# Sorting the tokens of three of ten blocks by expert, and taking a stage's order from a list schedule

## Chip, cores and metric

The kernel runs on one core of a Trainium2 chip. The metric is the time of one execution on the device in microseconds (us), as a median of several runs. Beside the runs there is one execution recorded by the hardware profiler: its span is the time from its first to its last instruction.

## What is computed

A network of four layers over 2500 nodes (padded to 2560 rows, 20 tiles of 128) of 256 features and 40000 edges: a relational graph layer, a mixture of 6 experts, a graph attention layer with a feed-forward part, and a mixture of 8 experts. Each is added to its input. The change touches the second layer and the stage that it shares with the first:

```python
# first layer, per edge: a row of a table by source node and edge type, summed by destination node
H = jnp.einsum('ni,rio->nro', x, W)
agg = jax.ops.segment_sum(H[src, etypes], dst, num_segments=N_NODES)
...
# second layer: top 2 of 6 experts per node, each expert three products of 256 x 256
rh = jax.nn.relu(features @ router_w1 + router_b1)
expert_logits = jax.nn.softmax(rh @ router_w2 + router_b2, axis=-1)
top_w, top_i = jax.lax.top_k(expert_logits, TOP_K)
routing_weights = jax.nn.softmax(top_w, axis=-1)
h1 = jax.nn.relu(jnp.einsum('bsd,edh->bseh', features, expert_w1) + expert_b1)
h2 = jax.nn.relu(jnp.einsum('bseh,ehf->bsef', h1, expert_w2) + expert_b2)
expert_out = jnp.einsum('bsef,efo->bseo', h2, expert_w3) + expert_b3
sel = jnp.take_along_axis(expert_out, top_i[:, :, :, None], axis=2)
combined = jnp.sum(sel * routing_weights[..., None], axis=2)
```

`features` is the normalized sum of the node's input and the first layer.

## The kernel before

The program runs stages one after the other with a barrier between them: loading, the table of the first layer (`stage_tables`), the stage of the change (`stage_sums_experts`), and the attention stage, which also holds the last experts. A second run of `stage_sums_experts` with `redo` stands behind a condition and does not happen on these inputs.

`stage_sums_experts` holds two streams of work on the same engines. The first is 79 groups of 4 tiles of 128 edges. For each tile POOL issues one indirect gather of 128 rows of 1 KB from the table in DRAM (L1149), into a ring of 16 tiles, four groups. PE multiplies each gathered tile by a 0/1 matrix of the destinations (L1466) into one PSUM bank, `psG`; below group 50 it also adds the last row of the group before (L1464, "follow"). ACT copies one half out of the bank (`odd`, L1400), DVE adds the other (`halves`, L1215), SP stores the sum to the table `agg` in DRAM (`store`). From group 50 on POOL joins the first row by a DMA that accumulates (L1144, `join`).

The second stream is ten blocks of 256 nodes. Block b can start when group 8(b+1) is stored (the last after group 78); `READY_AFTER` lists these groups. SP loads the block's sums, DVE normalizes (`norm`, `normed`, with ACT's `std` between), PE transposes (`turn`), and the router follows: `hidden`, `logits`, `gates` (softmax and top 2 on DVE and ACT), `gateT`, `bias`. The experts are dense: each of the 6 experts is applied to every token of the block, as pieces A, B and C (first, second and third product) of four products of 128x128 by 256 columns. In float32 each product stands in the trace as two PE records, so a piece is 8 records. ACT evicts A and B with bias and relu (L1387), DVE evicts C, weighted by the gate, into an accumulator (`sum_expert`, L1309). The block's tail normalizes twice (`post`, `post1`, `post2`), transposes (`turn2`), projects to queries, keys and values (`q`, L1517, one piece per tile), splits the queries into three bf16 parts (`high`, `rest`, `mid`, `low`) and stores.

Every engine works its queue in order. The order of the pieces on PE, DVE, ACT and SP is written out by hand: `BEGIN0` says at which group each block begins, `PACE0` how many groups one unit of its pattern lasts, and `BLOCK0` gives each piece a place in the pattern; `order0` sorts all pieces by the resulting place. POOL simply issues gathers and joins. PSUM is divided by use: `psG` one bank for the groups, `psW` two for router, turns and projections, `psH` three for A and B, `psC` two for C; the last block's second projection uses `psH`.

## Time and profile before

| | us |
|---|---|
| median of 3 runs | 1725.58 |
| lowest and highest run | 1723.24, 1728.3 |
| span of the profiled execution | 1668.6 |
| its PE busy | 1495.7 |
| its VectorE (DVE) busy | 1028.6 |
| its GpSimd (POOL) busy | 781.2 |
| its ScalarE (ACT) busy | 615.6 |

The profiled execution has no time of its own among the runs; its span lies 57.0 us under the median. Busy time is the time in which an engine had an instruction under way. PE is the matmul engine, PEld its weight loads, SP the engine that issues most DMAs. The clock of a stretch is what the throttle granted to PE, 1.00 for 2.4 GHz and 0.50 for 1.2 GHz. In a timeline a row is one instruction or a run of like ones, and the bracket behind it says how long the engine was idle ahead of it and what ended that.

### The profile page before, as it was taken

To read this page: it belongs to the slowest core of one execution; us is meant where nothing else is said; L and a number is where in the kernel's file an instruction comes from. 1 tells how busy PE (TensorE), PEld (TensorE's weight loads), DVE (VectorE), ACT (ScalarE), POOL (GpSimd) and SP (SyncE) were. 2 spreads that over 40 slices of the span, in tenths; PEclk is the share of its full clock that TensorE was granted. 3 is DMA by queue.
4 is the path that set the end of the run, shared out by engine and by line. 5 is a ranking of instruction groups with operands and counts; after the bars stand their busy time and mean duration, and the time that the engine had idled before them with its cause. 6 is when DMAs were issued, how large, how long until landed. Compare 5 with 4: busy or idle time off the path is not lost. (4 is left out here: it accounts for less than half of the span.)

```text
span 1668.6 us, 23723 instructions
## 1 busy us (share of the span) xinstructions
PE 1495.7 (90%) x6795; PEld 1005.9 (60%) x6795; DVE 1028.6 (62%) x2542; ACT 615.6 (37%) x1534; POOL 781.2 (47%) x738
## 2 busy tenths in 40 slices
PE   4999788999999999998356799999999999999996
PEld 2554314665666777777233467767766767767785
DVE  6543244345445555545388789898898888896432
ACT  3121002333234343443022355554555445555341
POOL 1100277646755777600378666574746556540000
PEclk9999857999999999999556699999999999999997
DMA  8448456546766566631487885665757565641100
GB/s 258 164 161 261 142 151 172 154 115 191 213 175 180 166 190 178 164 94 47 137 252 216 267 253 165 193 180 167 208 152 212 143 196 169 179 122 39 29 7 9
DMA packets 191573, 270.07 MB, mean 162 GB/s; under 512 B 28295, under 2 KB 156035, under 8 KB 188867
## 3 DMA queue, kind: packets, MB, share of 16 engines
q1 hardware_dynamic: 148419, 144.77, 27.7%
q0 software_dynamic: 43008, 123.61, 26.8%
q8 instruction: 60, 0.98, 0.2%
q14 instruction: 86, 0.70, 0.1%
HBM read 196.22 MB, written 72.06 MB: 161 GB/s over the span
## 5 line engine op out<-in xcount | busy, mean ns | idle before, releaser
L1890 POOL DMA_INDIRECT att_kv<-table_kv,g_srcI x314 | 368.5, 1174 | 246.4 <-issue 180.4
L1149 POOL DMA_INDIRECT ex_hg<-table_h,z_idx x314 | 316.7, 1008 | 150.2 <-issue 84.9
L2441 PE MATMUL att_psR<-g_mw,att_h 128*128 128x256 f32 x640 | 163.9, 403 | 1.0 <-ACT att_h L2259 1.0
L2414 PE MATMUL att_psR<-att_t,g_mw 128*128 128x256 f32 (+1 forms) x640 | 154.8, 387 | 0.1
L1466 PE MATMUL ex_psG<-ex_hg,ex_oh 128*42 128x256 f32 x628 | 134.6, 427 | 13.3 <-DMA ex_hg<-table_h,z_idx 7.2
L751 PE MATMUL tab_psH<-e_u,tab_xT 128*128 128x512 f32 x320 | 142.6, 598 | 4.3 <-DVE e_u L532 4.3
L2441 PEld LDWEIGHTS att_psR<-g_mw,att_h 128*128 128x128 f32 x640 | 124.7, 200 | 23.0 <-ACT att_h L2259 4.0
L1387 ACT ACTIVATE ex_h<-ex_psH,g_cols 128x256 f32<-128x256 f32 (+1 forms) x240 | 97.3, 464 | 93.8 <-PE ex_psH L1488 93.1
L2414 PEld LDWEIGHTS att_psR<-att_t,g_mw 128*128 128x128 f32 x640 | 121.2, 199 | 16.6 <-issue 2.6
L1882 POOL DMA_DIRECT2D table_o<-att_part x59 | 54.2, 919 | 161.9 <-DMA table_o<-att_part 90.5
L2301 PE MATMUL att_psG<-att_kv,att_oh 128*42 128x264 f32 x628 | 109.5, 431 | 13.7 <-DVE att_kv L1997 13.3
L1910 DVE TENSOR_TENSOR att_kv<-att_kv,att_epb 128x1024 f32<-128x1024 f32 x79 | 96.4, 1220 | 39.9 <-DMA att_kv<-table_kv,g_srcI 32.9
L1501 PE MATMUL ex_psC<-e_experts,ex_h 128*128 128x256 f32 x480 | 114.0, 384 | 0.0
L1488 PE MATMUL ex_psH<-ex_xT,e_experts 128*128 128x256 f32 (+1 forms) x480 | 113.8, 380 | 0.1
L1215 DVE TENSOR_TENSOR ex_part<-ex_psG,ex_odd 42x256 f32<-42x256 f32 x79 | 32.5, 411 | 130.6 <-ACT ex_odd L1400 130.4
L1488 PE MATMUL ex_psH<-ex_h,e_experts 128*128 128x256 f32 (+1 forms) x480 | 111.6, 377 | 0.0
L2259 ACT ACTIVATE att_h<-att_psR,g_cols 128x256 f32<-128x256 f32 (+1 forms) x160 | 66.2, 464 | 116.8 <-PE att_psR L2414 116.4
L2105 DVE SCALAR_TENSOR_TENSOR att_acc<-att_psR,att_gate,att_acc 128x256 f32<-128x256 f32 x160 | 69.5, 475 | 59.8 <-PE att_psR L2441 59.8
L751 PEld LDWEIGHTS tab_psH<-e_u,tab_xT 128*128 128x128 f32 x320 | 60.8, 192 | 74.3 <-issue 71.0
L1501 PEld LDWEIGHTS ex_psC<-e_experts,ex_h 128*128 128x128 f32 x480 | 88.9, 190 | 19.6 <-issue 7.2
L1997 DVE TENSOR_TENSOR att_kv<-att_kv,att_p 128x1024 f32<-128x1024 f32 x79 | 95.5, 1209 | 7.0 <-ACT att_p L2212 6.9
L1488 PEld LDWEIGHTS ex_psH<-ex_xT,e_experts 128*128 128x128 f32 x480 | 87.7, 190 | 17.6 <-issue 7.7
(308 smaller groups left out, 2465.1 us busy)
## 6 DMA issues: line engine op xcount, KB each, us to landing
table_h<-tab_hs SPq DMA_DIRECT2D x20, 1024.0 KB, 4.0
att_eft<-in_eft SPq DMA_DIRECT2D x158, 64.0 KB
ex_db<-table_dst SPq DMA_DIRECT2D x79, 126.0 KB
table_ohT<-ex_ohT SPq DMA_DIRECT2D x79, 126.0 KB
att_ohT<-table_ohT SPq DMA_DIRECT2D x79, 126.0 KB
table_oh<-ex_oh SPq DMA_DIRECT2D x79, 84.0 KB, 2.3
att_oh<-table_oh SPq DMA_DIRECT2D x79, 84.0 KB, 4.0
table_kv<-ex_qkv SPq DMA_DIRECT2D x10, 512.0 KB, 4.8
```

The source lines that it names most:

```text
L751: ins = nc.tensor.matmul(psH[:, c % 4, :], xT[:, b % 2, k, q * P:(q + 1) * P], Wr[:, k, j * 512:(j + 1) * 512], start=(k == 0), stop=(k == ...
L1149: nc.gpsimd.indirect_dma_start(hg[:, t % RING0, :], None, d.h[:, :], bass.IndirectOffsetOnAxis(ap=g.idx0[:, t:t + 1], axis=0)).then_inc(go ...
L1387: nc.scalar.activation((h1 if what == "A" else h2)[:, e % 2, o, 0:used(b)], psH[:, n % 3, o * BLK0:o * BLK0 + used(b)], ACT.Relu, bias=vec ...
L1466: ins = nc.tensor.matmul(psG[at:at + WG, 0:D], oh[:, i % 3, t % TP, :], hg[:, t % RING0, :], start=(t <= second), stop=(t >= tiles(i)[-1] ...
L1488: ins = nc.tensor.matmul(psH[:, n % 3, o * BLK0:o * BLK0 + w_], w[:, e, k, o * P:(o + 1) * P], x[:, k, 0:w_], start=(k == 0), stop=(k == D ...
L1501: ins = nc.tensor.matmul(psC[:, e % 2 * BT0 + q, :], h2[:, e % 2, k, q * P:(q + 1) * P], g.w3[:, e, k, :], start=(k == 0), stop=(k == DK - 1))
L1890: nc.gpsimd.indirect_dma_start(kv[:, t % (RINGC * TP), H:H + 2 * D], None, d.kv[:, :], bass.IndirectOffsetOnAxis(ap=g.srcI[:, t:t + 1], ax ...
L1910: nc.vector.tensor_tensor(k, k, epb[:, i % 2, :, :].unsqueeze(2).to_broadcast([P, TP, H, DH]), ALU.add).then_inc(s.added, 1)
L1997: nc.vector.tensor_tensor(kv[:, b:b + TP, 0:H * VW].rearrange("p t (a c) -> p t a c", c=VW)[:, :, :, 0:DH], kv[:, b:b + TP, H + D:H + 2 * ...
L2301: ins = nc.tensor.matmul(psG[at:at + WG, 0:H * VW], oh[:, i % 3, t % TP, :], kv[:, t % (RINGC * TP), 0:H * VW], start=(t <= second), stop= ...
L2414: ins = nc.tensor.matmul(out[:, c * CB:c * CB + used(b)], g.mw1[:, e, k, c * P:(c + 1) * P], t3[:, k, 0:used(b)], start=(k == 0), stop=(k ...
L2441: ins = nc.tensor.matmul(out[:, q * D:(q + 1) * D], h1[:, n % 3, k, q * P:(q + 1) * P], g.mw2[:, e, k, :], start=(k == 0), stop=(k == DK - 1))
```

## The change

Blocks 4, 5 and 6 no longer apply all six experts to all tokens. Their 768 tokens are each written twice, once for each chosen expert, into a table `sorted_x` in DRAM, sorted by expert: DVE marks the choices, PE counts them with products by a triangular and an all-ones matrix (`rank`), DVE makes positions (`pos`), and POOL scatters the normalized rows by indirect DMAs (`scatter`, four per block). The table is cut into 17 slots of 128 rows of one expert each, 2 x 768 / 128 + 6 - 1, the most that can be needed; all 17 always run. DVE makes a table of each slot's expert and first row (`table`), PE loads the expert numbers into registers (`experts`), SP loads the slots (`sL`). For each slot PE transposes the rows (`sX`), multiplies them by the expert's weights, addressed by the register (`sA`), transposes (`tA`), multiplies (`sB`), transposes (`tB`), multiplies (`sC`); ACT evicts the transposes, with bias and relu for `tA` and `tB`, and DVE evicts the products. SP stores each slot's result (`sS`) to `sorted_y`, POOL fetches for each token its two rows (`fetch`, four per block), and DVE adds them with their gates (`combine`). The table `sorted_x` is set to zero in the stage before, by DMAs of SP beside the stores of the first layer's table (5376 rows of 1 KB; two tiles of 128 rows at a time, eight at the last).

The other seven blocks stay dense, but C is added straight into `x` (`sum_expert`) and the mixed biases are added by DVE first (`mixed`); the accumulator and `addx` go. The gates are split into `shift`, `exp`, `choose`, `exp2` and `mix`.

PSUM is divided anew: five banks `psR` are handed out piece by piece for everything but the groups and the projections, which keep `psG` and `psW`; PE waits for the piece that held the bank before (`take`). The last block's projections have `psW` alone. The tile `u` is reused for sums (two deep), `u2` (two deep), the fetched rows and the loaded slots (four deep). The loads of destination rows (`db`) are three deep instead of two.

The order is no longer written by hand. `pieces0` gives each piece a cost, a rank and the pieces it needs; `plan0` puts them in order, always the piece that could start first, and among equals the lowest rank. POOL's order now comes from it too. SP's `store` is split into `store`, `keep` and `sums`.

```diff
+                    if tile >= 2:
+                        each = SXROWS // P // (NT - 2)
+                        n = each if tile < NT - 1 else SXROWS // P - (NT - 3) * each
+                        at = (tile - 2) * each * P
+                        sp.dma_start(d.sx[at:at + n * P, :].rearrange("(t p) c -> p t c", p=P),
+                                     zero[:, 0:D].unsqueeze(1).to_broadcast([P, n, D])).then_inc(cleared, 16)
...
+DENSE0, PARTS0 = (0, 1, 2, 3, 7, 8, 9), ((4, 5, 6),)
...
+SLOTS0 = [2 * cap // P + E0 - 1 for cap in CAP0]
...
+XR, YR, DB = 4, 2, 3
...
 
 
...
+COST0 = {"gather": 5.0, "join": 1.25, "scatter": 5.0, "fetch": 5.0,
+         "group": 1.66, "turn": 0.62, "hidden": 1.05, "logits": 0.52, "rank": 0.35, "gateT": 0.38, "bias": 0.90,
+         "experts": 1.20, "sX": 0.31, "sA": 0.96, "tA": 0.31, "sB": 0.96, "tB": 0.31, "sC": 0.96, "A": 1.90, "B": 1.90, "C": 1.90, "turn2": 0.62, "q": 2.90}
...
+RANK0 = {"route": 2.1, "slots": 7.5, "pace": 1.0, "dense": 45.6, "post": 59.2, "fetch": 4.4}
...
+        at = 8.0 * b + RANK0["dense"]
...
+            add("PE", "A", b, e, at + e, after("ACT", "turn", b), after("PE", "sC", AT0[slots_before[-1] + 1] - 1, slots_before[-1]) if slots_before else after("", "", -1))
...
+            add("PE", "B", b, e, at + e - 0.5, after("ACT", "A", b, e))
...
+            add("PE", "C", b, e, at + e - 0.7, after("ACT", "B", b, e))
...
+        at = 8.0 * part[-1] + RANK0["slots"]
...
+            add("SP", "sL", n, p, at + RANK0["pace"] * j, prior("PE", "sX", XR), after("DVE", "table", p), *(after("POOL", "scatter", b, 0, LANDS) for b in part))
+            add("PE", "sX", n, p, at + RANK0["pace"] * j - 0.3, after("SP", "sL", n, p, LANDS), prior("PE", "sX", 1), after("PE", "experts", p),
+                *(after("PE", "C", b, E0 - 1) for b in DENSE0 if b < part[0]))
+            add("ACT", "sX", n, p, at + RANK0["pace"] * j, after("PE", "sX", n, p), prior("PE", "sA", 2))
+            add("PE", "sA", n, p, at + RANK0["pace"] * j, after("ACT", "sX", n, p), prior("PE", "sA", 1))
...
+            add("PE", "tA", n, p, at + RANK0["pace"] * j - 0.5, after("DVE", "sA", n, p))
...
+            add("PE", "sB", n, p, at + RANK0["pace"] * j - 0.6, after("ACT", "tA", n, p), prior("PE", "sB", 1))
...
+            add("PE", "tB", n, p, at + RANK0["pace"] * j - 0.7, after("DVE", "sB", n, p))
...
+            add("PE", "sC", n, p, at + RANK0["pace"] * j - 0.8, after("ACT", "tB", n, p), prior("PE", "sC", 1))
+            add("DVE", "sC", n, p, at + RANK0["pace"] * j - 20.0, after("PE", "sC", n, p), prior("SP", "sS", YR, LANDS))
+            add("SP", "sS", n, p, at + RANK0["pace"] * j - 20.0, after("DVE", "sC", n, p))
...
+            add("POOL", "fetch", b, 0, at + RANK0["fetch"], *(after("SP", "sS", m, p, LANDS) for m in range(AT0[p], AT0[p + 1])),
...
+        best = None
+        for engine, pieces in open_.items():
+            for piece in pieces:
+                start = max(free[engine], ready[piece])
+                if engine == "PE" and piece[1] in HELD0:
+                    start = max(start, min(banks))
+                if start < float("inf") and (best is None or (start, work[piece][1]) < best[0]):
+                    best = ((start, work[piece][1]), piece)
...
+        engine, what, b, e = piece
...
+        end = free[engine] = start + work[piece][0]
+        orders[engine].append((what, b, e))
+        if engine == "PE" and what in HELD0:
+            n = min(range(5), key=lambda n: banks[n])
+            bank[what, b, e], behind[what, b, e] = n, holder[n]
...
+        sums_in = g.u[:, 0:2 * BT0, :].rearrange("p (a t) c -> p a t c", t=BT0)
+        u2 = g.u[:, 2 * BT0:4 * BT0, :].rearrange("p (a t) c -> p a t c", t=BT0)
+        yf = g.u[:, 4 * BT0:8 * BT0, :].rearrange("p (a t j) c -> p a t j c", t=BT0, j=2)
+        xs = g.u[:, 8 * BT0:8 * BT0 + XR, :]
...
-        psH = m.ps("psH", [P, 3, 512])
-        psC = m.ps("psC", [P, 2 * BT0, D])
...
+        psR = m.ps("psR", [P, 5, 512])
...
+                for p, part_of in enumerate(PARTS0):
+                    nc.gpsimd.iota(g.first0[:, p, :], [[CAP0[p], E0]], base=AREA0[p], channel_multiplier=0, allow_small_or_imprecise_dtypes=True)
+                    nc.gpsimd.iota(g.row0[:, AT0[p]:AT0[p + 1]], [[P, SLOTS0[p]]], base=AREA0[p], channel_multiplier=0,
+                                   allow_small_or_imprecise_dtypes=True)
+                nc.gpsimd.iota(g.turn0[:, :], [[1, SL]], base=0, channel_multiplier=0, allow_small_or_imprecise_dtypes=True).then_inc(s.places, 1)
...
+                def scatter(b):
+                    pool.wait_ge(s.pos_ready, sparse(b) + 1)
+                    pool.wait_ge(s.xn_ready, b + 1)
...
+                    for q in range(B0[b]):
+                        for j in range(2):
+                            nc.gpsimd.indirect_dma_start(d.sx[:, :], bass.IndirectOffsetOnAxis(ap=pos[:, T0[b] + q, j:j + 1], axis=0),
+                                                         xn[:, b % 2, q, :], None).then_inc(scattered[PART0[b]][b % 2], 16)
...
+                for what, b, e in orders["POOL"]:
+                    if what == "gather":
+                        if b * TP >= RING0:
+                            pool.wait_ge(s.summed, b - RING0 // TP + 1)
+                        for t in tiles(b):
+                            nc.gpsimd.indirect_dma_start(hg[:, t % RING0, :], None, d.h[:, :],
+                                                         bass.IndirectOffsetOnAxis(ap=g.idx0[:, t:t + 1], axis=0)).then_inc(got[t % RING0], 16)
+                    if what == "join":
...
+                def keep_first(n):
+                    dve.wait_ge(s.sa_made, n + 1)
+                    if n >= 2:
+                        dve.wait_ge(s.ta_made, n - 1)
+                    nc.vector.tensor_copy(ha[:, n % 2, :], psR[:, bank["sA", n, PART_OF[n]], 0:D]).then_inc(s.sa_kept, 1)
...
+                def take(what, b, e):
+
+                    if behind[what, b, e]:
+                        pe.wait_ge(*drained(*behind[what, b, e]))
+                    return None if what == "q" else psR[:, bank[what, b, e], :]
...
+                def turn_slot(what, n, p, src, made):
+                    out = take(what, n, p)
+                    for k in range(DK):
+                        ins = nc.tensor.transpose(out[:, k * P:(k + 1) * P], src[:, k * P:(k + 1) * P], g.ident[:, :])
+                    ins.then_inc(made, 1)
+
+                def layer_slot(what, n, p, x, w, made):
+                    out = take(what, n, p)
+                    for k in range(DK):
+                        ins = nc.tensor.matmul(out[:, 0:D], x[:, n % 2, k, :], w[:, ds(expert[n], 1), k, :].rearrange("p a c -> p (a c)"),
+                                               start=(k == 0), stop=(k == DK - 1))
+                    ins.then_inc(made, 1)
...
+                        if what == "sX":
+                            pe.wait_ge(x_got[b % XR], 16 * (b // XR + 1))
+                            turn_slot(what, b, e, xs[:, b % XR, :], s.xs_made)
+                        if what == "sA":
+                            pe.wait_ge(s.xs_ready, b + 1)
+                            layer_slot(what, b, e, xsT, g.w1, s.sa_made)
...
+                        if what == "sL":
+                            if b == AT0[e]:
+                                sp.wait_ge(s.table_ready, 3 * e + 1)
+                                for j in range(2):
+                                    sp.wait_ge(scattered[e][j], scatters(e, PARTS0[e][-1], j))
+                                settle(sp)
+                            at = sp.value_load(tabR[0:1, b:b + 1], min_val=0, max_val=SXROWS - P)
+                            if b >= XR:
+                                sp.wait_ge(s.xs_made, b - XR + 1)
+                            sp.dma_start(xs[:, b % XR, :], d.sx[ds(at, P), :]).then_inc(x_got[b % XR], 16)
+                        if what == "sS":
+                            sp.wait_ge(s.y_ready, b + 1)
+                            sp.dma_start(d.sy[e][(b - AT0[e]) * P:(b - AT0[e] + 1) * P, :], y[:, b % YR, :]).then_inc(y_stored[b % YR], 16)
```

## Rows read from the trace of the kernel before

**Rows 1.** The page: the span and the busy time of each engine.

```profile
span 1668.6 us, 23723 instructions
...
PE 1495.7 (90%) x6795; PEld 1005.9 (60%) x6795; DVE 1028.6 (62%) x2542; ACT 615.6 (37%) x1534; POOL 781.2 (47%) x738
```

**Rows 2.** Busy time of each engine in four stretches (window: length, engines with counts, clock, DMA).

```profile
core 0: us, PE busy (x) PEld busy (x) DVE busy (x) ACT busy (x) POOL busy (x), PEclk, DMA share, GB/s
220.00:240.00 20.00, 16.15 (x43) 4.11 (x44) 9.32 (x46) 1.48 (x4) 15.43 (x16) 0.50 0.59 154
275.00:700.00 425.00, 419.30 (x1966) 283.03 (x1965) 205.39 (x683) 156.87 (x361) 276.51 (x279) 1.00 0.60 172
700.00:790.00 90.00, 86.00 (x420) 69.44 (x418) 46.20 (x147) 36.81 (x86) 4.91 (x6) 1.00 0.25 76
790.00:800.00 10.00, 2.27 (x6) 1.38 (x7) 5.50 (x18) 1.61 (x4) 0.00 (x0) 0.70 0.15 52
```

**Rows 3.** Timeline of PE near 610 us (start, length, engine, line, operation, count).

```profile
604.92 1.07 PE L1466 MATMUL ex_psG<-ex_hg,ex_oh 128*42 128x256 f32 x8
605.91 1.99 PE L1501 MATMUL ex_psC<-e_experts,ex_h 128*128 128x256 f32 x8
607.74 0.60 PE L365 MATMUL ex_psW<-g_ident,ex_xn 128*128 128x128 f32 x4
...
617.40 1.99 PE L1488 MATMUL ex_psH<-ex_h,e_experts 128*128 128x256 f32 x8
619.23 1.89 PE L1488 MATMUL ex_psH<-ex_xT,e_experts 128*128 128x256 f32 x8
```

**Rows 4.** Timeline of PE near 400 us: a group below 50, and what follows it.

```profile
400.06 1.06 PE L1466 MATMUL ex_psG<-ex_hg,ex_oh 128*42 128x256 f32 x6
...
402.13 1.99 PE L1488 MATMUL ex_psH<-ex_xT,e_experts 128*128 128x256 f32 x8
```

**Rows 5.** Timeline of POOL: the iota, the first and the fiftieth gather of the stage.

```profile
194.31 0.93 POOL L1134 IOTA ex_qrow<- 128x126 f32 x1 [46.94 <-POOLq L813]
195.41 1.32 POOL L1149 DMA_INDIRECT ex_hg<-table_h,z_idx  x1 [0.17 <-issue]
...
261.03 1.51 POOL L1149 DMA_INDIRECT ex_hg<-table_h,z_idx  x1 [0.30 <-issue]
```

**Rows 6.** DMA issues by tensor (count, size of one, median us to landing).

```profile
table_h<-tab_hs SPq DMA_DIRECT2D x20, 1024.0 KB, 4.0
...
ex_hg<-table_h,z_idx POOLq DMA_INDIRECT x314, 3.6
...
att_x<-table_x SPq DMA_DIRECT2D x10, 256.0 KB, 3.3
```

**Rows 7.** Timelines of ACT, PE and DVE: routing of the first and of the last block.

```profile
249.25 0.37 ACT L1400 COPY ex_odd<-ex_psG 42x256 f32<-42x256 f32 x1 [4.89 <-PE ex_psG L1466]
...
264.76 1.06 PE L365 MATMUL ex_psW<-g_ident,ex_xn 128*128 128x128 f32 x4
...
748.06 0.60 PE L365 MATMUL ex_psW<-g_ident,ex_xn 128*128 128x128 f32 x4
...
754.69 0.17 DVE L933 TENSOR_TENSOR ex_r_p<-ex_psW,g_rows 128x12 f32<-128x12 f32 x1 [0.79 <-PE ex_psW L1573]
...
759.50 0.16 DVE L1258 TENSOR_TENSOR ex_r_m<-ex_r_m 128x2 f32<-128x2 f32 x1
```

**Rows 8.** Timeline of PE: the end of the stage.

```profile
786.22 3.62 PE L1501 MATMUL ex_psC<-e_experts,ex_h 128*128 128x256 f32 x16
796.53 1.12 PE L365 MATMUL ex_psW<-g_ident,ex_xn 128*128 128x128 f32 x4 [6.69 <-DVE ex_xn L1231]
798.85 5.46 PE L1517 MATMUL ex_psW<-z_wqkv,ex_x2T 128*128 128x512 f32 x8 [1.20 <-ACT ex_x2T L1433]
804.10 2.79 PE L1517 MATMUL ex_psH<-z_wqkv,ex_x2T 128*128 128x512 f32 x8
```

748 lines of the change are left out of this document (570 added, 178 removed), and 5 rows, old and new, of the table BLOCK0.

## The prediction

> **What bounds the kernel now.** I read four views in this order. The page gives a span of 1668.6 us with PE busy 90% of it, the next engine at 62% [rows 1], so the question is where PE works and where it waits. Busy time by stretch answers it for the stage that the change rewrites, which runs from about 194 us (first iota) to about 817 us: from 275 to 700 us PE is busy 419.3 of 425 us, from 700 to 790 us 86.0 of 90 us, both at clock 1.00 (2.4 GHz) [rows 2]. So this stage is bound by PE's work from 275 us on, with 9.7 us of holes in 515. Ahead of 275 us PE waits for gathers: in 220 to 240 us it does groups alone at clock 0.50 (1.2 GHz), while POOL issues one gather after the other [rows 2]. Behind 790 us the last block's chain runs through DVE and ACT, and PE has 2.3 us of work in 10 us. Stretches outside this stage are untouched but for zero stores in the stage ahead of it. The third view, PE's timeline, prices the pieces; the fourth, POOL's timeline with the landings of transfers, says when a block can start.
>
> The median of the runs is 1725.58 us, 57.0 us above the span; I carry those 57 us over unchanged and sum against the span.
>
> **What the change takes from PE.** A dense piece is 8 records and goes from start to start in 1.83 us: a C from 605.91 to 607.74, a B from 617.40 to 619.23 [rows 3]. A block has 18 of them, 32.9 us; three blocks lose 98.8 us.
>
> **What it adds to PE.** Seventeen slots, each three layers of 4 records (half of 1.83, 0.92 us) and three turns of 2 transposes (half of the 0.60 us of four [rows 3], 0.30 us): 3.66 us, 62.2 us for all. Operands addressed by a register are not in the trace. From below they cost nothing, since the address could be resolved while the array streams; from above I take 0.3 us per layer piece, the pause that a POOL instruction shows ahead of itself without waiting for anything (0.30 <-issue [rows 5]), 15 us in all. I take 0, because PE's records here follow each other without a gap [rows 3] and the address is known long before. Three rankings and the load of 17 expert numbers are some 2.4 us (a ranking is shorter than a group's 0.99 us, 604.92 to 605.91; 0 to 5 us). Net PE work: -98.8 + 62.2 + 2.4 = **-34.2 us**. Routing, biases, projections and groups stay.
>
> **The start.** Three iotas go ahead of the first gather; the present one takes 0.93 us and 0.17 us pass after it [rows 5]. Three like it are 3.3 us; they are shorter, 17 columns at most, so I take **+2.2 us** (1 to 3.3). This stretch waits for POOL, so it counts in full.
>
> **The hole before the slots.** Slots share their buffers with the dense blocks, so no slot starts before block 3's last C, and no A of block 7 before the last slot's sC. And none starts before block 6, the third of the part, is sorted. Two times must be compared.
>
> When does PE run out of dense work? Groups have rank i and dense block 0 rank 45.6, so PE takes a group whenever one is ready. A group below 50 holds PE 2.07 us (400.06 to 402.13 [rows 4]), a later one 0.99 us. The fiftieth gather starts at 261.03, the first at 195.41, 1.34 us apart [rows 5]; from 220 to 240 us there are 16, 1.25 us apart [rows 2]. A group's four are 5.0 to 5.4 us; I take 5.3. Group 49 lands near 195.4 + 2.2 + 50 x 5.3 + 3.6 = 466 us (3.6 us to landing [rows 6]). From 275 us PE has 1 - 2.07/5.3 = 61% for blocks, 116 us until then. Four blocks need 4 x 42.3 us: 32.9 dense, 6.2 for the tail (four transposes 0.60, two projections of 2.79 [rows 3, 8]), some 3.2 for routing, an estimate from the same pieces. With the routing of blocks 4 and 5 that is 175 us. The remaining 59 us run at 84% (0.99 us per 6.3 us, a join of 1.2 added): dense work ends near **537 us**.
>
> When can the first slot start? Group 56 needs 57 x 5.3 = 302 us of gathers, the scatters of blocks 4 and 5 (eight indirect issues, priced as gathers, 10.6 us) and three joins (3.7 us): it lands near 518 us with its PE work. From a group's odd half to block 0's turn it took 15.5 us (249.25 to 264.76 [rows 7]), part of it behind other DVE work, and a join adds some 4 us: 17.5 us. Turn to logits took 6.6 us beside other pieces (748.06 to 754.69), alone some 3.8; the gate's choice takes 5.0 us (754.69 to 759.66 [rows 7]); ranking and positions 2; the scatter 5.3 and 3.6 to land; the slot's load 0.4 and 3.3 [rows 6]. Together 40 us: **558 us**.
>
> The gap is 21 us, in which groups (16%) and block 6's own routing (3.3 us) occupy PE: **+15 us** idle, from 0 (dense work 4% dearer and the chain 5 us shorter close it) to 30 (the slower pieces of each pair).
>
> Behind the hole the slot pipeline fills: a slot passes PE, ACT and DVE six times in turn, so the first gives PE some 5 us of holes, **+5 us** (2 to 10). PE's clock falls in such holes: after 6.69 us of idle the projection at 798.85 took 5.46 us, the next one 2.79 [rows 8], **+2.7 us**. The Trainium skill, "TensorE: Matmul & The Clock Gate", section "What's actually happening", says that the throttled clock is the default and that activity releases it; rows 2 and 8 agree (0.50 with groups alone, 0.70 over the end). [...]
>
> **The order.** PE's holes were 1.3% from 275 to 700 us and 4.4% from 700 to 790 [rows 2]. The new order comes from a list of fixed costs that puts each piece where it is just ready, with no slack: 5.0 us for four gathers against 5.3 here, 1.66 us for each group against 2.07 and 0.99. I take 3% of 480 us, 14.5 against 9.7: **+5 us** (-4 to +15). New waits sit here: a scatter waits on POOL with all later gathers behind it, the first slot's load waits on SP with stores and sums behind it. Both have four groups of ring and four partial sums in front; if that cover is gone a late scatter delays the next group one for one.
>
> **The end.** Block 8's tail has rank 123.2, behind all of block 9's dense pieces (122.6 at most), so its projections (5.6 us) can fall into the 6.69 us in which PE waited for the last block's norm, and the last projection then finds a fast clock (2.7). Against it, the last block has no second projection bank any more: its second projection waits some 1.2 us for DVE. **-6 us** (-8 to +1.2).
>
> **Counted as nothing:** 5.5 MB of zeros in the stage ahead, beside PE, whose h stores of 1 MB land in 4.0 us [rows 6]; the last zero store is 1 MB, so up to 4 us if it queues in front of the last h store. DVE's and ACT's 51 small evictions each and 12 fetches on POOL lie beside PE; DVE was busy 205 of 425 us, ACT 157 [rows 2].
>
> Sum: -34.2 + 2.2 + 15 + 5 + 2.7 + 5 - 6 = **-10.3 us**, 1725.6 - 10.3 = **1715.3 us**; span near 1658.
>
> **Rivals.** *No hole.* If block 6 is sorted when block 3 ends, 15 and 2.7 us go: -28 us, **1697 us**. For it: the two times are 21 us apart out of 540, and 0.2 us per group closes half. Against: the 5.3 us per group were measured with PE and DVE at light work.
>
> *Groups late (slower than before).* The hole grows if groups come later than each 5.3 us; each 0.1 us is 5.7 us on block 6 and 4.8 us of PE idle, since PE runs out at nearly the same time. From 5.5 us per group on nothing is gained. From 275 to 700 us POOL ran 279 instructions [rows 2], some 26 of them joins: 63 groups, 6.7 us each, but there PE was the limit. At 5.9 us the sum is +18 us: **1744 us**. For it: each group waits for ACT's odd half and DVE's sum before the next may use its one bank, and both queues hold long pieces now.
>
> *Slots bound by hand-overs.* If a slot takes 4.6 us instead of 3.66, because bank, ACT copy and DVE copy don't come in time, or because registers cost their upper bound, 15 to 16 us come back: **1731 us**, about no change. For it: two buffers per step. Against: five banks, and groups and tails to fill in.
>
> *The work isn't cut*: were experts so uneven that 17 slots did not hold all tokens, the kernel would be wrong; 17 is the most that can be needed, and all 17 always run, so this can't move the time.
>
> **Chances.** Forecast 0.45, no hole 0.19, groups late 0.21, hand-overs 0.15. A measurement tells 0.3% (5.2 us) from no change. Faster takes 0.39 of the forecast, all of no hole and 0.02 of hand-overs: 0.60. Within 0.3%: 0.05, 0.03 of groups late, 0.07 of hand-overs: 0.15. Slower: 0.25. The range reaches from no hole with a clean order, 1694, to groups late, 1745; the forecast's own is 1704 to 1726.
>
> **What would show it.** PE has some 120 records fewer (432 dense gone, 204 layer and 102 turn records and a few more added). The hole: PE idle or at a clock below 1.00 somewhere in 530 to 570 us, ended by a slot's transpose waiting for its load. Groups: the 57th group's gather near 515 us. Slots: 17 in 62 to 75 us. The end: the stage over near 807 instead of 817 us, its last projection at 2.8 us. The prediction is wrong if the hole is elsewhere, for instance at each group, or if PE waits at pieces whose order the list put too early.

## The result and the profile after

| | before | changed |
|---|---|---|
| median of the runs, us | 1724.41 (4 runs) | 1773.66 (4 runs) |
| lowest and highest run | 1707.03, 1728.3 | 1767.1, 1777.17 |
| span of the profiled execution | 1668.6 [rows 1] | 1772.6 |
| its time as a run | none | 1775.16 |

The ratio is 1.0307 (95% interval 1.0262 to 1.0351): some 49 us slower where 10 us faster was forecast, and outside the range of 1694 to 1745. The page of the changed kernel, against [rows 1]: PE has about as much modelled work as before (1501.1 us against 1495.7) and a longer span.

```profile
span 1772.6 us, 24123 instructions
...
PE 1501.1 (85%) x6676; PEld 995.1 (56%) x6676; DVE 1050.6 (59%) x2630; ACT 611.2 (34%) x1539; POOL 791.5 (45%) x765
```

Its busy time by stretch, against [rows 2]: from 275 to 700 us PE works 364 of 425 us instead of 419, at clock 0.92 instead of 1.00.

```profile
core 0: us, PE busy (x) PEld busy (x) DVE busy (x) ACT busy (x) POOL busy (x), PEclk, DMA share, GB/s
220.00:240.00 20.00, 5.25 (x16) 1.68 (x17) 5.91 (x28) 0.74 (x2) 11.79 (x13) 0.50 0.37 109
275.00:700.00 425.00, 364.26 (x1597) 223.16 (x1595) 192.75 (x696) 129.27 (x307) 262.71 (x271) 0.92 0.61 173
700.00:890.00 190.00, 164.47 (x746) 124.50 (x744) 94.42 (x275) 64.32 (x156) 44.82 (x47) 0.94 0.32 95
```

POOL's timeline of the changed kernel gives the stage's length, from the first iota to the first gather of the attention stage: 704.6 us. In the first trace of the kernel before it is 623 us (194.31, [rows 5], to 817.55).

```profile
194.84 0.94 POOL L1364 IOTA ex_qrow<- 128x126 f32 x1 [46.94 <-POOLq L833]
...
899.46 1.07 POOL L2417 DMA_INDIRECT att_kv<-table_kv,g_srcI  x1 [120.57 <-issue]
```

So by the traces the stage is 81 us longer, but by the runs the program is only 49 us longer. That mismatch was the first thing to settle.

### The profile page after: what moved, and what is told of

Same layout as the page of the kernel before. It is cut to its first block and busy times, and to the rows that moved or that the text cites. A ratio compares the mean times of both kernels' runs of the same rounds, so it can differ in the third digit from the quotient of the medians.

```text
span 1772.6 us, 24123 instructions
## 1 busy us (share of the span) xinstructions
PE 1501.1 (85%) x6676; PEld 995.1 (56%) x6676; DVE 1050.6 (59%) x2630; ACT 611.2 (34%) x1539; POOL 791.5 (45%) x765
## 5 line engine op out<-in xcount | busy, mean ns | idle before, releaser
L2417 POOL DMA_INDIRECT att_kv<-table_kv,g_srcI x314 | 363.9, 1159 | 298.0 <-issue 209.8
L1407 POOL DMA_INDIRECT ex_hg<-table_h,z_idx x314 | 308.1, 981 | 185.0 <-PE ex_psG L1936 83.3
L1936 PE MATMUL ex_psG<-ex_hg,ex_oh 128*42 128x256 f32 x628 | 140.2, 439 | 54.1 <-issue 47.8
L1835 ACT ACTIVATE ex_h<-ex_psR,g_cols 128x256 f32<-128x256 f32 (+1 forms) x168 | 69.1, 463 | 152.5 <-PE ex_psR L1951 77.0
L1936 PEld LDWEIGHTS ex_psG<-ex_hg,ex_oh 128*42 128x42 f32 x628 | 44.8, 127 | 128.6 <-issue 108.3
L1951 PE MATMUL ex_psR<-ex_h,e_experts 128*128 128x256 f32 (+1 forms) x336 | 85.5, 402 | 22.7 <-ACT ex_h L1835 21.4
L2442 DVE TENSOR_TENSOR att_kv<-att_kv,att_psQ 128x1024 f32<-128x1024 f32 x79 | 95.3, 1206 | 13.5 <-DMA ex_db<-table_dst 13.4
L1848 ACT COPY ex_odd<-ex_psG 42x256 f32<-42x256 f32 x79 | 29.1, 369 | 211.3 <-PE ex_psG L1936 112.8
L1424 DVE TENSOR_TENSOR ex_oh<-g_iotag,g_dstgrp 128x168 f32<-128x168 f32 x79 | 25.7, 328 | 120.4 <-PE ex_psG L1936 52.8
L2448 DVE TENSOR_REDUCE att_S<-att_kv 128x32 f32<-128x1024 f32 x79 | 95.5, 1209 | 0.9
```

The lines of the kernel that those rows point to most:

```text
L1407: nc.gpsimd.indirect_dma_start(hg[:, t % RING0, :], None, d.h[:, :], bass.IndirectOffsetOnAxis(ap=g.idx0[:, t:t + 1], axis=0)).then_inc(go ...
L1936: ins = nc.tensor.matmul(psG[at:at + WG, 0:D], oh[:, i % 3, t % TP, :], hg[:, t % RING0, :], start=(t <= second), stop=(t >= tiles(i)[-1] ...
L2417: nc.gpsimd.indirect_dma_start(kv[:, t % (RINGC * TP), H:H + 2 * D], None, d.kv[:, :], bass.IndirectOffsetOnAxis(ap=g.srcI[:, t:t + 1], ax ...
L2442: nc.vector.tensor_tensor(keys(i), keys(i), psQ[:, :, :], ALU.mult).then_inc(s.product, 1)
L2448: nc.vector.tensor_reduce(heads(i), keys(i).rearrange("p t (a c) -> p t a c", c=DH), AX.X, ALU.add).then_inc(s.reduced, 1)
```

## Experiments

All ratios are to the kernel before, run on the same chip beside the kernel. The rows come from five chips, on which the kernel before had medians of 1722.7 to 1730.7 us, so a difference of a few us between rows of different chips says little by itself; the ratio then tells more.

| run | median us | ratio, 95% interval | stage us |
|---|---|---|---|
| kernel before, again | 1730.86 (one run) | | 661.0 |
| changed kernel, again | 1779.49 (one run) | | 707.5 |
| list alone (all dense) | 1753.38 | 1.0209, 1.0139 to 1.0279 | 687.0 |
| halves first | 1765.5 | 1.0256, 1.0188 to 1.0325 | 702.0 |
| halves first, prices by shape | 1757.66 | 1.0147, 1.0107 to 1.0187 | 694.4 |
| list alone, both of these | 1747.51 | 1.0118, 1.0067 to 1.0170 | 679.5 |
| slots late (blocks 6 to 8) | 1762.16 | 1.0182, 1.0148 to 1.0217 | 696.5 |
| slots late, both of these | 1738.93 | 1.0059, 1.0023 to 1.0094 | 665.0 |
| the same with two group banks | 1738.71 | 1.0072, 1.0036 to 1.0109 | 677.0 |
| two banks, blocks 7 and 8 sorted | 1732.13 | 1.0026, 0.9997 to 1.0055 | 672.9 |
| two banks, list alone | 1743.89 | 1.0085, 1.0040 to 1.0130 | 680.1 |
| one bank, blocks 7 and 8 sorted | 1723.81 | 1.0006, 0.9974 to 1.0038 | 651.9 |
| before, plain loads, first run | 1680.08 (one run) | | 607.8 |
| before, plain loads | 1679.17 | 0.9724, 0.9665 to 0.9782 | 611.4 |
| changed, plain loads | 1674.6 | 0.9692, 0.9638 to 0.9745 | 612.3 |
| list alone, plain loads | 1697.42 | 0.9813, 0.9748 to 0.9878 | 627.2 |
| slots late and both, plain loads | 1649.79 | 0.9549, 0.9480 to 0.9617 | 585.8 |

### Both kernels once more

No edit.

> The kernel before once more, unchanged, for a second trace of it: the first one has a span of 1668.6 us under a median of runs of 1725. If that first execution was an unusually quick one, the span here is near 1705 to 1725 us and the stage of sums and experts lasts longer than its 623 us (194 to 817). If not, the span is again near 1669 and 55 us lie outside it. In the trace of the changed kernel 102 signals of PE in this stage reach their reader over 0.3 us after the modelled end of the matmul (3.0 us on average), in the first trace of the kernel before none of 421. If late signals are a property of the executions, they are here too, and with them holes of PE of some 40 us more; if they come from the change, there are none.

> The changed kernel once more, unchanged. First trace: stage from 194 to about 895 us, PE holes of 160 us in it, first slot at 638.4, one hole of 12.6 us at 232 and one of 13 us at 755, 102 late signals of PE. If these holes belong to the order of the pieces, they come again at the same places (2.5 us at each group from 239 to 288, 10 us at the second product of the first dense block behind the slots); if they belong to that execution, they are elsewhere or gone. Time 1767 to 1777 us either way.

The second trace of the kernel before has a span of 1729.3 us in a run of 1730.86: 1.6 us lie outside it, not 57. Its page, its stretches and POOL's two rows:

```profile
span 1729.3 us, 23723 instructions
...
220.00:240.00 20.00, 8.99 (x24) 2.48 (x24) 6.06 (x29) 0.96 (x3) 12.20 (x13) 0.50 0.40 111
275.00:700.00 425.00, 402.31 (x1826) 264.86 (x1825) 191.27 (x638) 143.37 (x330) 253.89 (x255) 0.97 0.57 160
700.00:800.00 100.00, 95.86 (x470) 75.06 (x468) 54.17 (x186) 41.66 (x98) 30.99 (x33) 1.00 0.42 125
...
193.87 0.93 POOL L1134 IOTA ex_qrow<- 128x126 f32 x1 [46.92 <-POOLq L813]
...
854.90 1.08 POOL L1890 DMA_INDIRECT att_kv<-table_kv,g_srcI  x1 [92.96 <-issue]
```

The stage lasts 661 us here, 38 more than in the first trace, and the attention stage 874 instead of 851. From 275 to 700 us PE stands 22.7 us, where [rows 2] have 5.7. The first trace was of an execution whose span is some 36 us shorter than the shortest that a timed run of that kernel has (1704.5). The fair difference between the stages is 706 - 661 = 45 us, close to the 49 of the medians.

Where PE stands shows in timelines, first PE and ACT of the kernel before, second trace. A group ends at 468.81 + 0.63 = 469.44 us; ACT, idle, takes its odd half only at 472.35.

```profile
468.81 0.63 PE L1466 MATMUL ex_psG<-ex_hg,ex_oh 128*42 128x256 f32 x2
469.37 1.99 PE L1488 MATMUL ex_psH<-ex_xT,e_experts 128*128 128x256 f32 x8
471.20 1.89 PE L1501 MATMUL ex_psC<-e_experts,ex_h 128*128 128x256 f32 x8
...
472.35 0.37 ACT L1400 COPY ex_odd<-ex_psG 42x256 f32<-42x256 f32 x1 [5.83 <-DMA table_x<-e_x]
```

PE's signal came 2.9 us late, and PE lost nothing, because the hand-written order gave it an A and a C in between. The same in the changed kernel: a group ends at 484.25 + 0.63 = 484.88, ACT takes its half at 488.59, 3.7 us late ("remote": the signal came long after its sender's end).

```profile
484.25 0.63 PE L1936 MATMUL ex_psG<-ex_hg,ex_oh 128*42 128x256 f32 x2
485.88 1.99 PE L1951 MATMUL ex_psR<-ex_h,e_experts 128*128 128x256 f32 x8 [1.01 <-issue]
489.61 1.07 PE L1936 MATMUL ex_psG<-ex_hg,ex_oh 128*42 128x256 f32 x6 [1.74 <-issue]
...
484.99 0.84 ACT L1835 ACTIVATE ex_h<-ex_psR,g_cols 128x256 f32<-128x256 f32 x2 [3.70 <-remote]
488.59 0.37 ACT L1848 COPY ex_odd<-ex_psG 42x256 f32<-42x256 f32 x1 [2.76 <-remote]
...
489.10 0.41 DVE L1476 TENSOR_TENSOR ex_part<-ex_psG,ex_odd 42x256 f32<-42x256 f32 x1
```

Here PE stands twice, 1.01 and 1.74 us: the list has put the B right behind the relu it needs, and the next group right behind the sum that frees the bank. I call a signal late when an engine's signal comes over 0.3 us (and under 9 us) after the modelled end of the matmul that sends it and its reader starts on it. Counted over the stage: none of 421 in the first trace of before, 71 in the second, 102 and 104 in the two of the changed kernel, 3 to 4 us late on average. In the attention stage, which is the same in both programs: none in the first trace of before, 93, 81 and 92 in the others. These counts depend on how the reader is told (another way gives 62 and 112 where 71 and 102 stand), but none stays none. The holes of the changed kernel returned (some 121 and 122 us from PE's first to its last instruction of the stage, against 67 in the second trace of before), with the 2.5 us at each group in the same place.

The traces with late signals differ from the others in one more way: they lack records of signals. From 275 to 700 us the engines' instructions raise semaphores 1248 times in the first trace of before, and it has 1244 such records; in the second it is 717 of 1155, in the changed kernel 685 of 1162. From 40 to 194 us, where no signal is late, none lacks any. So in these stretches "issue" and "remote" behind a wait can also mean that the sender's record is missing, and the idle time and the start of the reader are the surer evidence. Whether recording has a part in the delay, or one cause makes both, no run tells; the timed runs show the longer time.

### The list alone, and one part of its order

```diff
-DENSE0, PARTS0 = (0, 1, 2, 3, 7, 8, 9), ((4, 5, 6),)
+DENSE0, PARTS0 = tuple(range(10)), ()
```

> The list schedule alone: all ten blocks dense, no sorting, no slots, no scatter and no fetch; the zero stores and one of the three iotas stay. Theory (the order costs the time, the slots are worth what they were meant to be): PE gets 34 us more work than in the changed kernel and the same holes at the groups, so it is slower than before by more than the changed kernel is, +55 to +85 us, 1780 to 1810. Rival (the slots cost more than the dense work that they save): about the kernel before, -5 to +15 us. Rival between (half and half): +25 us.

It is 1753.4, some 30 us over the kernel before beside it (stage 687 against 661), 20 under the changed kernel: near the rival between (+25). The list costs some 30 us, the slots another 20.

```diff
-add("DVE", "prepare", i, 0, at, after("PE", "group", i if i <= NSG // 2 else i - 1), ...
+add("DVE", "prepare", i, 0, at, after("DVE", "halves", i) if i <= NSG // 2 else after("PE", "group", i - 1), ...
-add("PE", "group", i, ... after("DVE", "prepare", i - 1 if i <= NSG // 2 else i - 2))
+add("PE", "group", i, ... after("DVE", "prepare", i - 2))
```

> The changed kernel, but for the first eleven groups DVE adds the halves of a group before it prepares the masks and node ids of the next one; the groups wait only for the windows that they read. In the trace PE stands 2.54 us at each of the groups 3 to 11 while DVE works 2.2 us on masks ahead of the sum that frees the bank. Theory (order, zero slack): the period of a group from 232 to 290 us falls from 7.04 to about 5.5 us, group 10 comes 10 to 15 us sooner, and the time falls by 5 to 15 us against the changed kernel (1759 to 1769), less than the gain at group 10 because the later order has its own holes. Rival (these groups only wait for gathers anyway): no change in the period beyond 0.3 us and none in the time.

First the changed kernel's timelines of PE and DVE at a group of the start. PE ends the group's node ids at 243.07 + 0.69 and stands 2.54 us; DVE works through the masks from 243.58, and the sum that frees the bank comes last, at 245.79.

```profile
243.07 0.69 PE L1923 MATMUL ex_psR<-g_ident,ex_rep 128*128 128x128 f32 x2
246.29 1.94 PE L1936 MATMUL ex_psG<-ex_hg,ex_oh 128*42 128x256 f32 x6 [2.54 <-issue]
...
243.58 0.44 DVE L1431 COPY ex_rep<-g_dstF 128x128 f32<-128x128 f32 x2 [4.19 <-PE ex_psR L1923]
...
245.52 0.35 DVE L1450 TENSOR_SCALAR ex_mk<-ex_ne 128x127 bf16<-128x127 f32 x2
245.79 0.41 DVE L1476 TENSOR_TENSOR ex_part<-ex_psG,ex_odd 42x256 f32<-42x256 f32 x1
```

With the halves first the same group (the one numbered 5) starts after 0.34 us, and groups 4 to 9 follow each other in 3.8 us instead of 7.0; the hole of 12.85 us ahead of group 4 stays, as the changed kernel has one of 12.58 ahead of group 3:

```profile
237.27 1.94 PE L1936 MATMUL ex_psG<-ex_hg,ex_oh 128*42 128x256 f32 x6 [12.85 <-issue]
...
242.11 1.94 PE L1936 MATMUL ex_psG<-ex_hg,ex_oh 128*42 128x256 f32 x6 [0.34 <-issue]
```

Group 10 ended 16 us sooner (268.1 instead of 284.6 us); the median fell by 8 us, within what was expected, though the intervals of the two ratios overlap. The rest of the gain went into later holes: the stage has no fewer in sum (127 us).

### Prices, and the place of the slots

The plan has one price for a group (1.66 us) and one for preparing (0.80). Those are means over unlike shapes: a group below 50 takes 2.07 us [rows 4], a later one 0.99 [rows 3]; preparing with masks takes 2.2 us and more.

```diff
+if what == "group":
+    cost = (4.0 if b < 13 else 2.07 if b < JOINED_FROM else 1.05) + (0.7 if 1 <= b <= NSG // 2 else 0.0)
+if what == "prepare":
+    cost = 2.5 if b <= NSG // 2 else 0.35 if b < TABLES_FROM else 0.80
+if what == "gather":
+    cost = 5.2
```

> The changed kernel with the halves first, and with prices of the plan by shape instead of one mean per kind: a group 4.0 us for the first 13 (half clock), 2.07 below 50, 1.05 above, and 0.7 for the node ids of the first ten; preparing 2.5 us up to group 10, 0.35 up to 16, 0.80 behind; four gathers 5.2. Theory (the plan's mean prices put PE's pieces where they are not ready): 15 to 25 us less than the changed kernel's 1774, 1749 to 1759, and the waits of PE at the groups fall from 54 to under 35 us. Rival (late signals between engines make the holes, whatever the prices): within 5 us of the run with the halves first, 1760 to 1771.

> The list schedule alone, all ten blocks dense, with the halves first and the prices by shape. Theory of the prices: 1725 to 1738, within 1% of the kernel before, so that the list schedule itself costs next to nothing once its prices are right. Rival of the late signals: 1743 to 1755, as the list schedule alone with mean prices (1753).

With prices by shape 8 us less than with the halves first by the medians (from 2.6% to 1.5% behind by the ratios). That lies in the theory's range near its upper end, but its sign failed: PE's waits ahead of group records fell from 54 to 45 us, not under 35. The list alone gained 6 us, in its rival's range, and stays 1.2% behind. So prices matter, and are not the main thing.

```diff
-DENSE0, PARTS0 = (0, 1, 2, 3, 7, 8, 9), ((4, 5, 6),)
+DENSE0, PARTS0 = (0, 1, 2, 3, 4, 5, 9), ((6, 7, 8),)
```

> The changed kernel with blocks 6, 7 and 8 sorted instead of 4, 5 and 6, nothing else: the slots then run behind the last gather. In the traces of the changed kernel a slot takes PE 4.6 us instead of 3.7, and PE stands some 43 us between 600 and 800 us, where the list schedule with dense blocks alone stands 4 us. Theory (a slot is a chain of six hand-overs, and signals between engines come late while gathers run, 20 a 50 us there and none behind the last gather): PE's work of a slot falls to 3.7 to 4.1 us, the holes around the slots to under 25 us, the time by 10 to 25 us, 1749 to 1764. Rival (the slots lose by the wait for sorting and their own chain, wherever they stand): 1768 to 1785.

> Both: blocks 6, 7 and 8 sorted, halves first, prices by shape. If both theories hold: 1720 to 1740, no slower than the kernel before or faster by up to 5 us. If only the prices matter: 1749 to 1759. If only the place of the slots matters: 1745 to 1760. If neither: above 1760.

The slots of blocks 6 to 8 run behind the last gather (708 us; first slot at 752). PE's groups by line, first the changed kernel over its slots (625 to 720 us, where some records of the layers lie outside), then the late ones: layers and transposes shrink a little (4.2 us a slot, just over the 3.7 to 4.1 expected), the waits ahead of the slots' records fall from some 17 us to 1.

```profile
L1990 PE MATMUL ex_psR<-e_experts,ex_h 128*128 x179 | 47.2, 399 | 9.1 <-ACT ex_h L1886 5.1 <-issue 2.2 <-ACT ex_h L1895 1.8
L1984 PE MATMUL ex_psR<-g_ident,e_u 128*128 128x128 f32 x34 | 7.4, 310 | 5.1 <-DMA e_u<-sorted_x 4.0 <-issue 1.1
```

```profile
L1990 PE MATMUL ex_psR<-e_experts,ex_h 128*128 x204 | 52.4, 382 | 0.8 <-ACT ex_h L1895 0.8
L1984 PE MATMUL ex_psR<-g_ident,e_u 128*128 128x128 f32 x34 | 6.5, 274 | 0.0
```

Late alone gains 12 us on the changed kernel, late with halves and prices 35: 1738.9, 0.6% behind the kernel before and 9 us ahead of the list alone with the same prices. A slot is a chain of six hand-overs. With halves first and prices by shape it pays behind the gathers (9 us ahead of the list alone) and doesn't among them (10 us behind); with the mean prices the late slots are only level with the list alone (ratios 1.0182 and 1.0209).

### A second bank for the groups

The groups get two PSUM banks, the others four instead of five; a group waits for the sum of the group before last to begin, and for the last one only ahead of its "follow" record.

```diff
-                    if i >= 1:
-                        pe.wait_ge(s.part_ready, i)
+                    if i >= 2:
+                        pe.wait_ge(s.part_ready, i - 1)
...
+                            pe.wait_ge(s.part_ready, i)
                             nc.tensor.matmul(psG[0:1, i % 2, 0:D], g.follow[0:WG, i - 1:i], ...
```

> Blocks 6, 7 and 8 sorted, halves first, prices by shape, and two PSUM banks for the groups instead of one (four instead of five to hand out): a group may begin while ACT and DVE still take the group before out of the other bank; only its last two records wait for that sum. In that kernel with one bank PE stood 47.3 us ahead of group records. Theory (with one bank each group waits for PE to ACT to DVE to PE, and the list puts the next group right at the end of that chain, so each late signal is a hole): those 47 us fall to 15 to 30, the stage by 12 to 25 us, time 1715 to 1727, below the kernel before. Rival (PE waits for gathers there, or the list fills in other work anyway): 1733 to 1745.

> As with two banks, but only blocks 7 and 8 sorted (13 slots, 8 blocks dense): the wait for sorting the last block of the part falls behind more dense work. PE gets 32.9 us more of dense work and 4 slots less (17 us): +16 us of work, and loses some 12 us of hole ahead of the slots. Within 6 us of the kernel with three blocks sorted; more than 10 us slower would say that sorting pays by its work alone, more than 10 us faster that the wait for sorting is the larger part.

> The list schedule alone (all blocks dense), halves first, prices by shape, two banks. With one bank it took 1747.5. Theory of the one-bank chain: 1725 to 1737, as the kernel before or up to 10 us over it. Rival: 1742 to 1752.

This theory fell: 1738.7 against 1738.9, and the list alone with two banks, 1743.9, is in its rival's range. PE by line, one bank and then two (the groups' records and the "follow"):

```profile
L1942 PE MATMUL ex_psG<-ex_hg,ex_oh 128*42 128x256 f32 x628 | 135.3, 431 | 47.3 <-issue 26.7 <-DVE ex_oh L1430 9.4 <-DMA ex_hg<-table_h,z_idx 7.5
L1940 PE MATMUL ex_psG<-ex_part,g_follow 42*1 42x256 f32 x98 | 33.5, 426 | 0.0
```

```profile
L1943 PE MATMUL ex_psG<-ex_hg,ex_oh 128*42 128x256 f32 x628 | 135.0, 428 | 5.8 <-DMA ex_hg<-table_h,z_idx 3.8 <-issue 1.8
L1941 PE MATMUL ex_psG<-ex_part,g_follow 42*1 42x256 f32 x98 | 33.1, 422 | 34.1 <-DVE ex_part L1482 18.0 <-issue 16.0
```

The bank's wait did fall, from 47 to 6 us, and came back as 34 us ahead of "follow", which needs the same sum: the chain, not the bank, is what PE waits for there. The others lost a bank by the same edit, and what that cost was not tried apart. With two banks, blocks 7 and 8 sorted gave 1732.1, as expected within 6 us, with the rest as before.

> Halves first, prices by shape, one bank for the groups, blocks 7 and 8 sorted, gathers as they are. With three blocks (6 to 8) sorted it took 1738.9, with two banks and blocks 7 and 8 sorted 1732.1. If the second bank changed nothing, as it did for three blocks: 1726 to 1736, about the kernel before (1729). Below 1722 would be a version that beats both.

Blocks 7 and 8 sorted, one bank: 1723.8, between the two ranges that were set, and no difference from the kernel before beside it (1722.7) that can be measured. No version with the gathers as they are beat it.

### Plain loads in place of the gathers

```diff
-nc.gpsimd.indirect_dma_start(hg[:, t % RING0, :], None, d.h[:, :],
-                             bass.IndirectOffsetOnAxis(ap=g.idx0[:, t:t + 1], axis=0)).then_inc(got[t % RING0], 16)
+nc.gpsimd.dma_start(hg[:, t % RING0, :], d.h[t % 160 * P:(t % 160 + 1) * P, :]).then_inc(got[t % RING0], 16)
```

> The kernel before with POOL's indirect gathers of the first layer replaced by plain loads of the same size, issued by POOL at the same places (so the sums are of wrong rows; the attention stage keeps its gathers). In its second trace 71 signals of PE in this stage come over 0.3 us late and 93 in the attention stage, none in the stages without gathers. If the indirect addressing goes with the late signals, this stage has none or few here, the attention stage its 80 to 95, and the stage gets shorter by up to 38 us (661 to 623). If the traffic alone does it, the stage has its 60 to 80.

> The kernel before with plain loads for the first layer's gathers (sums of wrong rows), once more and over rounds, as the mark for the next three: about 1680 us, no late signals in the stage.

> The changed kernel with plain loads at the places of the gathers (sums of wrong rows; scatters and fetches stay indirect), so that hardly any signal comes late in its stage. The changed kernel is 49 us slower than the kernel before. If the late signals, which the first trace of the kernel before didn't have, make most of that, the changed kernel is here within 15 us of 1680, 1665 to 1695, as the sum of the prediction had it. If the order and its prices do, it stays 30 us or more behind, above 1710.

> The list schedule alone (all dense, mean prices) with plain loads. With gathers it is 28 us behind the kernel before and 20 us ahead of the changed kernel. If late signals make its loss: 1675 to 1692. If the mean prices and the preparing ahead of the sum do: 1700 to 1712. And if the slots need signals in time, they pay here: the changed kernel is 10 to 25 us under this one instead of 20 over it.

> Blocks 6, 7 and 8 sorted, halves first, prices by shape, with plain loads. With gathers it is 10 us behind the kernel before. If signals in time let the list and the slots show their worth: 1655 to 1672, 8 to 25 us under the kernel before with plain loads. If not: 1680 to 1695.

The loads now take rows in their order, so the sums are of other rows; the sizes and the places are the same. The first run gave 1680.1 us, no late signal in the stage, 94 in the attention stage of the same execution. The trace lacks no record of a signal in this stage (1246 of 1246 from 275 to 700 us in the row "before, plain loads"), and lacks some in the attention stage (439 of 623 from 900 to 1100 us). ACT's waits from 290 to 700 us, kernel before (second trace), with plain loads, and the first trace of all: in the first, many of the waits for a group's end can't be laid to the group any more, as its signal is late or its record is missing; in the other two nearly all can.

```profile
ACT ex_odd L1400 <- PE ex_psG L1466: 54.1, 29, 6.7
...
ACT ex_odd L1400 <- DMA table_x<-e_x: 28.6, 6, 7.4
ACT ex_odd L1400 <- issue: 21.7, 9, 4.8
```

```profile
ACT ex_odd L1399 <- PE ex_psG L1465: 93.7, 46, 6.7
```

```profile
ACT ex_odd L1400 <- PE ex_psG L1466: 91.7, 46, 6.7
```

With plain loads in all four kernels: before 1679.2, changed 1674.6, list alone 1697.4, late slots with halves and prices 1649.8. The changed kernel is 4.6 us under the kernel before instead of 49 over it (not clear of noise: 0.9692 and 0.9724, with intervals that overlap), and 23 us under the list alone instead of 20 over it; the mended one is 29 us under, more than was expected. The list alone lies between its two ranges. The stretches of PE, before and changed:

```profile
275.00:680.00 405.00, 399.93 (x1875) 268.91 (x1875) 194.89 (x644) 147.98 (x340) 151.47 (x265) 1.00 0.59 173
```

```profile
275.00:650.00 375.00, 358.78 (x1725) 231.00 (x1725) 195.53 (x698) 140.00 (x338) 166.42 (x286) 0.97 0.68 205
```

This replaces more than the signals: POOL is busy 151 us of 405 instead of 254 of 425, and groups can come sooner. For the kernel before the two can be told apart by its first trace, which has the gathers and no late signal: its stage takes 623 us, against 661 with late signals and 611 with plain loads. So of the 50 us some 38 go with the late signals and 12 with the loads. The changed kernel has no such trace. That is why the second mark is needed: all four kernels get it, and what remains between them is the order and the slots. The scatters and fetches stayed indirect, with a handful of late signals (4) in the changed kernel's stage. What the runs show is that the change loses with the gathers and doesn't lose without them; that in the changed kernel the late signals are what carries this, and not POOL's slower issue, rests on the holes at single hand-overs above and on that split, and was not tried apart.

## Why the prediction was wrong, step by step

In one sum: PE stands 67 us in the stage of the second trace of before and 121 in the changed kernel's, 54 more, where the terms for holes (+15, +5, +5 and -6) make 19. Its work, as the traces model it with the clock that it had, falls by 8 us (582 to 574), not by 34.2. The step that failed is the pricing of the waits: the 57 us, the holes of the order and the 5.3 us per group all came from a trace without late signals. The work term was missed as well.

**The 57 us "carried over unchanged".** This step failed first. They did not lie outside the span: the second span is 60.7 us longer, 38 of it in this stage and 23 in the attention stage, and 1.6 us lie outside. I read a quick execution as the rule, and with it "PE's records here follow each other without a gap" and "9.7 us of holes in 515". A gap of 57 us between median and span, where the first to last instruction is what a run consists of, was a reason to doubt the trace, not a constant to carry.

**The rival that was nearest.** "Groups late" named the mechanism, a group waiting for ACT's odd half and DVE's sum before the next may use its bank, and the point from which it decides, 5.5 us per group. It was priced at 5.9 us; from group 10 to group 56 the changed kernel took 6.5 us each (with plain loads 5.5). The sum stands at 5.3 us; at 4.8 us for each 0.1 us, 6.5 would be 58 us on top of it, +47, which is what was measured. That is in part luck: the kernel before takes 6.6 us for each of these groups in its quick trace and 7.2 in the second, so a pace of 6.5 alone makes no loss; the rival's price holds only where PE runs out of other work. The cause, signals that come late, stood in neither the trace nor the text.

**The hole before the slots.** Forecast: first slot at 558 us. PE's timeline of the changed kernel has it at 638.4, that of the changed kernel with plain loads at 568.7, each ended by the load of sorted rows:

```profile
638.41 0.44 PE L1984 MATMUL ex_psR<-g_ident,e_u 128*128 128x128 f32 x2 [3.95 <-DMA e_u<-sorted_x]
```

```profile
568.71 1.49 PE L1983 MATMUL ex_psR<-g_ident,e_u 128*128 128x128 f32 x6 [4.75 <-DMA e_u<-sorted_x]
```

So the comparison of times held where signals came in time; PE's largest single wait in that hole was 4 to 5 us, and part of the forecast 15 was filled by groups and tails. With the gathers the first slot came 80 us later than forecast, 21 of them already there at group 10 (281 instead of some 260 us by the same 5.3).

**PE's work.** The slots took 55.8 us for layers and 21.2 for turns, 77 instead of 62.2: 4.5 us a slot. In time and behind the gathers they take 4.1 to 4.3. A layer's record takes 0.26 us of the slots' time (52.4 us for 204) and not the 0.23 us of a running piece: the term was some 10 us too small, and the other 5 come only where the slots stand among the gathers (clock 0.89 from 600 to 745 us). The rest of the 26 us by which the work misses its term isn't laid to single pieces; the clock from 275 to 700 us is 0.92, against 0.97 in the second trace of before. Operands addressed by a register left no pause that shows, 0.1 us of waits ahead of 204 records with plain loads, so the value taken there is borne out as far as waits go; whether they have a part in the longer record was not tried.

```profile
L1989 PE MATMUL ex_psR<-e_experts,ex_h 128*128 x204 | 52.4, 391 | 0.1
```

**The order.** Taken at +5 (-4 to +15) us of holes. The list alone has 87 us of holes in the stage against 67 (second trace of before), and some 30 us more time; with plain loads 45 against 38, 7 us of holes, but 18 us more time. There PE works longer at half clock at the start (from 240 to 275 us clock 0.50, against 0.72 in the kernel before with plain loads); that the mean prices and the preparing ahead of the sum make this is likely by the runs above and was not tried with plain loads. The range held for holes only where signals come in time, and the start's order was not read at all: that prepare stands ahead of halves could be seen in the change's own dependencies.

**The start.** +2.2 us for three iotas was too dear: from the first iota to the first gather 1.42 us (194.84 to 196.26) instead of 1.10 [rows 5], +0.3.

**The end.** As forecast the very last projection is quick, but not the one before it, and the second of each pair waits 1.24 us for DVE, as the text said of the last (PE's timeline, against [rows 8]). Such a short hole doesn't slow what follows (2.82 us); behind holes of 1.90 and 1.52 us the projection took 4.54:

```profile
874.81 2.82 PE L2002 MATMUL ex_psW<-z_wqkv,ex_x2T 128*128 128x512 f32 x8 [1.24 <-DVE ex_qkv L1749]
879.53 0.66 PE L368 MATMUL ex_psR<-g_ident,ex_xn 128*128 128x128 f32 x4 [1.90 <-DVE ex_xn L1492]
881.70 4.54 PE L2002 MATMUL ex_psW<-z_wqkv,ex_x2T 128*128 128x512 f32 x8 [1.52 <-ACT ex_x2T L1903]
887.49 2.82 PE L2002 MATMUL ex_psW<-z_wqkv,ex_x2T 128*128 128x512 f32 x8 [1.24 <-DVE ex_qkv L1749]
```

PE's wait for the last norm is 1.90 us instead of 6.69.

**What was right.** With plain loads, where signals come in time, the forecast's -10.3 us stands beside -4.6. That is closer than the terms deserve: the traces' stages are equal (612.3 and 611.4 us), PE's work falls by 19 us instead of 34, and the holes grow by 21. So there the holes came near their terms, and the work did not. It was not the case that was run. The text's own test, "the prediction is wrong if the hole is elsewhere, for instance at each group, or if PE waits at pieces whose order the list put too early", is what the trace shows.

## What to carry to other kernels

Look whether the profiled execution stands among the runs before arguing from its gaps; a second trace of the same program costs little and here changed 5.7 us of PE's holes into 22.7. An order with no slack between a result and its reader is only as good as the signals between engines: price each hand-over with the lateness that the runs have, put long chains of small steps where nothing disturbs them, and keep independent work between a piece and the next that needs its result. A list schedule's prices belong to shapes, not to kinds.

## What the runs showed of the hardware

- In this stage, with indirect gathers on POOL, some 60 to 120 of PE's signals were late in each of its traces but the first, by 3 to 4 us on average; from 40 to 194 us none was, and behind the last gather at most 4. With plain loads of the same size (DMA 0.59 busy, 173 GB/s, against 0.57 and 160 with gathers) none came late in that stage and 94 in the next one, which kept its gathers. DVE's and ACT's signals were late too (some 130 and 30 over the second trace of the kernel before).
- Late ones often arrive together. In the changed kernel signals of PE due at 463.51 and 465.59 us came at 469.23 and 469.34, and ACT and DVE, both idle for over 6 us, began at 469.25 and 469.36:

```profile
464.96 0.63 PE L1936 MATMUL ex_psG<-ex_hg,ex_oh 128*42 128x256 f32 x2
470.14 1.22 PE L1951 MATMUL ex_psR<-ex_h,e_experts 128*128 128x256 f32 x2 [4.56 <-ACT ex_h L1835]
...
469.25 0.84 ACT L1835 ACTIVATE ex_h<-ex_psR,g_cols 128x256 f32<-128x256 f32 x2 [6.73 <-remote]
...
469.36 0.33 DVE L1424 TENSOR_TENSOR ex_oh<-g_iotag,g_dstgrp 128x168 f32<-128x168 f32 x1 [6.29 <-remote]
```

- Where signals came late, records of signals are missing from the trace too (of the kernel before from 275 to 700 us, 717 of 1155 are there in the second trace, 1244 of 1248 in the first). A wait's releaser is then often not told.
- Gathers alone don't suffice: the first trace of the kernel before had the same gathers, no late signal of PE and hardly a missing record. What makes an execution quiet, what path the signals share with indirect addressing, and whether recording has a part was not tried and stays open.
- The Trainium skill, "TensorE: Matmul & The Clock Gate", section "The cost: per-tile semaphore tail", puts the tail of semaphore increments, where every tile's matmul makes one, at 26.3 ns for each. No run here measures that tail: the records of signals that aren't late stand 0.01 us (median) behind the matmul's modelled end, and late ones of 3 to 4 us are over a hundred times the page's figure.
